# A graph and mixture-of-experts block on one core: places inside the inner products, both turns between the outer products, shared outer products evicted by ScalarE

## What is computed

```python
probs = jax.nn.softmax(flat @ Wr, axis=-1)            # flat: the normalized x, 625 by 768; 8 experts
topk_p, topk_i = jax.lax.top_k(probs, 2)
...
order = jnp.argsort(-score, axis=1)[:, :capacity]     # of each expert, its 196 best nodes
dispatch = flat[order]
gate = jax.nn.silu(jnp.einsum('ech,ehi->eci', dispatch, w1))     # 768 by 192 of each expert
up = jnp.einsum('ech,ehi->eci', dispatch, w3)
expert_out = jnp.einsum('eci,eih->ech', gate * up, w2)
...
shared = jax.nn.silu(flat @ s1) * (flat @ s3) @ s2
out = routed + shared
```

## Time and profile before

| | us |
|---|---|
| median of three runs | 1425.12 |
| the profiled execution's own time | 1431.91 |
| its span | 1430.3 |
| TensorE busy | 1311.4 |
| VectorE busy | 964.7 |
| ScalarE busy | 556.2 |
| GpSimd busy | 642.4 |
| mean granted TensorE clock, share of full | 0.946 |

### The profile page before, as it was taken

How to read it: one execution, slowest core, us unless ns; L and a number is a source line. 1 busy time by engine, 2 the same in 40 slices (tenths; PEclk the granted TensorE clock), 3 DMA queues, 4 the chain that set the end, 5 groups by cost and what they waited for, 6 DMA issues and landing times.

```text
span 1430.3 us, 22837 instructions
## 1 busy us (share of the span) xinstructions
PE 1311.4 (92%) x7548; PEld 1114.4 (78%) x7548; DVE 964.7 (67%) x2158; ACT 556.2 (39%) x652; POOL 642.4 (45%) x564
## 2 busy tenths in 40 slices
PE   7988678899999979999999999999999769988997
PEld 5765578556997769999999999999867559765665
DVE  8967998878689645565666656565168765477634
ACT  1010575231432044545454545454157551212221
POOL 7025777777666533344344434443368720001112
PEclk9999688999999889999999999999999889988988
DMA  7950000020740338787878787878588843416745
GB/s 174 87 46 6 2 2 2 1 67 3 215 96 2 101 135 293 259 279 272 279 279 288 264 291 263 300 252 280 132 282 279 281 152 96 133 32 167 178 118 173
DMA packets 116403, 234.59 MB, mean 164 GB/s; under 512 B 36931, under 2 KB 57087, under 8 KB 116301
## 3 DMA queue, kind: packets, MB, share of 16 engines
q1 hardware_dynamic: 80780, 126.83, 31.0%
q0 software_dynamic: 22352, 70.40, 17.4%
q10 hardware_dynamic: 13200, 36.46, 6.9%
HBM read 195.26 MB, written 39.70 MB: 164 GB/s over the span
## 4 chain that ended last, share of the span: by engine, by line
PE 63%; DVE 24%; issue 5%; DMA 4%; ACT 3%; POOL 1%; another core or an unknown queue 0%; DVEq 0%; ACTq 0%; SPq 0%; POOLq 0%
PE PS L2722 30%; PE PS L2387 4%; PE PS L2712 3%; PE PS L3007 3%; PE PS L2598 3%; PE PS L2996 3%; DVE e L1320 3%; DVE mlo L2162 3%; PE PS L2855 2%; PE PS L2897 2%; PE PS L2785 2%; DVE e L1562 2%; DVE e L1599 2%; PE PS L2817 1%; PE PS L2906 1%
## 5 line engine op out<-in xcount | busy, mean ns | idle before, releaser
L814 POOL DMA_INDIRECT xg<-xn_dram,xrow x70 | 116.1, 1658 | 277.6 <-DVEq L1529 245.4
L2722 PE MATMUL PS<-whi,xhi 128*128 128x384 f32 x840 | 220.7, 343 | 1.0 <-ACTq L1102 1.0
L2722 PE MATMUL PS<-whi,xlo 128*128 128x384 f32 x840 | 214.7, 336 | 0.0
L2722 PE MATMUL PS<-wlo,xhi 128*128 128x384 f32 x840 | 213.1, 335 | 0.0
L1320 DVE TENSOR_TENSOR wlo<-raw,whi 128x2304 fp32r<-128x2304 f32 x68 | 175.2, 2576 | 38.0 <-ACTq L1085 31.5
L1083 ACT ACTIVATE whi<-raw 128x2304 fp32r<-128x2304 f32 x68 | 145.1, 2133 | 22.8 <-PE PS L2694 7.8
L2722 PEld LDWEIGHTS PS<-wlo,xhi 128*128 128x128 f32 x840 | 151.8, 188 | 0.0
L2722 PEld LDWEIGHTS PS<-whi,xlo 128*128 128x128 f32 x840 | 151.7, 188 | 0.0
L1320 DVE TENSOR_TENSOR xlo<-PS,xhi 128x768 fp32r<-128x768 f32 x70 | 67.0, 958 | 124.1 <-ACTq L1094 117.2
L2722 PEld LDWEIGHTS PS<-whi,xhi 128*128 128x128 f32 x840 | 148.3, 189 | 1.3 <-issue 1.3
L782 POOL DMA_INDIRECT evwb<-inv_dram,idxb x80 | 108.2, 1352 | 30.5 <-issue 22.4
(11 more groups left out here) (463 smaller groups left out, 2671.2 us busy)
## 6 DMA issues: line engine op xcount, KB each, us to landing
raw<-in_L_gnn_W_rel SPq DMA_DIRECT2D x68, 1152.0 KB
z_dram<-xn ACTq DMA_DIRECT2D x70, 384.0 KB, 7.3
gw<-in_L_gnn_W SPq DMA_DIRECT2D x2, 2304.0 KB, 27.4
fw<-in_L_ffn_w SPq DMA_DIRECT2D x8, 576.0 KB
fw<-in_L_ffn_w ACTq DMA_DIRECT2D x1, 4608.0 KB
y_dram<-yb ACTq DMA_DIRECT2D x14, 294.0 KB
xn_dram<-xn SPq DMA_DIRECT2D x10, 384.0 KB
wroot<-in_L_ffn_w SPq DMA_DIRECT2D x5, 576.0 KB, 5.0
```

The costliest lines, as they stand in the source:

```text
L814: pool.indirect_dma_start(xg[b][j][:, :], None, xn_dram, bass.IndirectOffsetOnAxis(ap=xrow[:, b, j:j + 1], axis=0)).then_inc(x_gathered[b] ...
L2722: mm = pe.matmul(slot(q)[:, s * BANK:s * BANK + HALF], a[:, k, :], wt[:, k, s * HALF:(s + 1) * HALF], start=(k == 0 and part == 0), stop=( ...
```

## The change

- Before the experts, ScalarE loads Exp's table by an activation whose result nobody uses. The router's columns of the tiles 3 and 4 are made between the shared inner products.
- ScalarE evicts the shared outer products into `xn` (`shared_out`), and VectorE adds them to x from there, one in each of the experts 1 to 5.
- VectorE ranks expert n+2, not n+3, while expert n runs. Spreads run three experts ahead.
- In every expert the places of e+1 are made inside the inner product of e, ahead of its third part. The spread, and for the experts 5 and 6 `turn_hots`, stands between inner product and outer product 0. Both turns of e+1 stand between the two outer products, the first in slot 0, the second in slot 3.
- `row_tables` and `add_lower` are both done in expert 6. In the last stretch, `last_low(0)` comes before the first two `add_higher`.

```diff
--- before.py
+++ after.py
@@ -64,7 +64,9 @@
 SH = T
 HT = CAP // 2
 RING = 3
-SPREAD_AHEAD = 4
+SPREAD_AHEAD = 3
+X_SLOT = (0, 3)
+SHARED_SLOT = (0, 1, 2, 1, 2)
 LOGITS_WITH = 3
 PLACES = 768
 FINAL = NE - 1
...
@@ -1224,7 +1227,7 @@
 
             def take_x(n, j):
                 act.wait_ge(turned, n * RT + j + 1)
-                step.do(act.activation(fxT[n % 2][:, :, j * HT:(j + 1) * HT], columns2(0)[:, :, 0:HT], ACT.Copy))
+                step.do(act.activation(fxT[n % 2][:, :, j * HT:(j + 1) * HT], columns2(X_SLOT[j])[:, :, 0:HT], ACT.Copy))
                 act.sem_inc(x_taken, 1)
 
             def y_out(n, j):
@@ -1271,43 +1274,48 @@
                 step.do(act.activation(hhT[t % 2][:, :, 0:P], slot(3)[0:HC, BANK + 256:2 * BANK].rearrange("p (c n) -> p c n", c=2)[:, :, 0:P], ACT.Copy))
                 act.sem_inc(hT_ready, 1)
 
+            def shared_out(t):
+                act.wait_ge(outer_full, t + 1)
+                step.do(act.activation(xn[:, t, :].rearrange("p (b c) -> p b c", b=2),
+                                       slot(SHARED_SLOT[t]).rearrange("p (b c) -> p b c", c=BANK)[0:P, :, 0:HALF], ACT.Copy))
+                act.sem_inc(outer_taken, 1)
+
             for t in range(LOGITS_WITH):
                 shared_gate(t)
+            act.activation(table_of_exp[:, :], ones[0:P, 0:1], ACT.Exp)
             shared_turned(0)
             router(2)
             shared_gate(3)
             shared_turned(1)
+            score_row(0)
+            act.wait_ge(xn_stored, 32 * T)
+            shared_out(0)
             shared_gate(4)
-            score_row(0)
             shared_turned(2)
+            shared_out(1)
             shared_turned(3)
+            shared_out(2)
             score_row(1)
+            shared_out(3)
             shared_turned(4)
-            score_row(2)
             for j in range(RT):
                 take_x(0, j)
+            shared_out(4)
             for n in range(NE):
                 expert_gates(n)
-                if n < 2:
-                    if n == 1:
-                        score_row(4)
-                    for j in range(RT):
-                        y_out(n, j)
-                        take_x(n + 1, j)
-                    score_row(3 if n == 0 else n + SPREAD_AHEAD)
-                    continue
-                if n + 1 < NE:
-                    take_x(n + 1, 0)
+                if n == 0:
+                    score_row(2)
+                if n + SPREAD_AHEAD < NE:
+                    score_row(n + SPREAD_AHEAD)
+                elif FINAL - RT <= n < FINAL:
+                    hot_out(n - (FINAL - RT))
                 if n == FINAL:
                     for j in range(RT):
                         y_last(j)
                     continue
                 y_out(n, 0)
-                take_x(n + 1, 1)
-                if n + SPREAD_AHEAD < NE:
-                    score_row(n + SPREAD_AHEAD)
-                elif n >= FINAL - RT:
-                    hot_out(n - (FINAL - RT))
+                for j in range(RT):
+                    take_x(n + 1, j)
                 y_out(n, 1)
 
 
@@ -2206,13 +2214,9 @@
                 do(dve.tensor_copy(scol[e % 2][:, :], score[:, :, e]))
                 dve.sem_inc(scol_ready, 1)
 
-            SHARED_SLOT = (0, 1, 2, 1, 2)
-
             def add_shared(t):
-                dve.wait_ge(outer_full, t + 1)
-                xr = x_res[:, t, :].rearrange("p (b c) -> p b c", b=2)
-                do(tt(xr, slot(SHARED_SLOT[t]).rearrange("p (b c) -> p b c", c=BANK)[0:P, :, 0:HALF], xr, ALU.add))
-                dve.sem_inc(outer_taken, 1)
+                dve.wait_ge(outer_taken, t + 1)
+                do(tt(x_res[:, t, :], xn[:, t, :], x_res[:, t, :], ALU.add))
 
             def rank(e, first, end):
 
@@ -2291,51 +2295,28 @@
                 column2(e)
             do(dve.memset(level[:, 0, :], 0.0))
             shared_hidden(3)
-            shared_hidden(4)
             dve.wait_ge(earlier_ready, 1)
             rank(0, 0, 3)
-            add_shared(0)
-            add_shared(1)
+            shared_hidden(4)
             rank(0, 3, T)
             placed(0)
-            add_shared(2)
             rows2(0)
-            rank(1, 0, 2)
-            add_shared(3)
-            rank(1, 2, 4)
-            add_shared(4)
-            rank(1, 4, T)
+            rank(1, 0, T)
             placed(1)
-            hidden_rest(0)
-            hidden_first(0)
-            rows2(1)
-            rank(2, 0, T)
-            placed(2)
-            rank(3, 0, 3)
-            hidden_rest(1)
-            rows2(2)
-            hidden_first(1)
-            rank(3, 3, T)
-            placed(3)
-            rank(4, 0, 3)
-            rows2(3)
-            rank(4, 3, T)
-            placed(4)
             do(dve.tensor_copy(ident16[:, :], ident[0:P, 0:P]))
-            for n in range(2, NE):
-                if n == FINAL:
+            for n in range(NE):
+                hidden_rest(n)
+                if n + 1 < NE:
+                    rows2(n + 1)
+                hidden_first(n)
+                if n + 2 < NE:
+                    rank(n + 2, 0, T)
+                    placed(n + 2)
+                    if 0 < n:
+                        add_shared(n - 1)
+                elif n + 2 == NE:
+                    row_tables()
                     add_lower()
-                hidden_rest(n)
-                hidden_first(n)
-                if n + 3 < NE:
-                    rank(n + 3, 0, 3)
-                if n + 2 < NE:
-                    rows2(n + 2)
-                if n + 3 < NE:
-                    rank(n + 3, 3, T)
-                    placed(n + 3)
-                elif n + 3 == NE:
-                    row_tables()
 
             def add_higher(t):
                 dve.wait_ge(y_gathered[max(t - 1, 0)], 32 if t < 2 else 16)
@@ -2347,13 +2328,12 @@
                 lanes = lambda a: a[0:HT, :].rearrange("p (b c) -> p b c", b=2)
                 tt(lanes(y_split[1][j]), of, lanes(y_split[0][j]).bitcast(f32), ALU.subtract).then_inc(y_lo, 1)
 
+            last_low(0)
             add_higher(0)
             add_higher(1)
-            last_low(0)
-            add_higher(2)
             last_low(1)
-            add_higher(3)
-            add_higher(4)
+            for t in range(2, T):
+                add_higher(t)
             for t in range(T):
                 dve.wait_ge(joined, t + 1)
                 xr = x_res[:, t, :].rearrange("p (b c) -> p b c", b=2)
@@ -2907,15 +2887,15 @@
                                    start=(k == 0), stop=(k == K - 1))
                 mm.then_inc(inner_full, 1)
 
-            def last_logits():
+            def logits_alone(t):
                 pe.wait_ge(free[3], BEFORE["slot3"][3])
-                for t in range(LOGITS_WITH, T):
-                    pe.wait_ge(xT_ready, XT_TURNED[5] + t + 1)
-                    c = (t - LOGITS_WITH) * NE
-                    for k in range(K):
-                        mm = pe.matmul(slot(3)[0:P, c:c + NE], xT[:, k, t * P:(t + 1) * P], s13[:, k, 2 * F:2 * F + NE],
-                                       start=(k == 0), stop=(k == K - 1))
-                mm.then_inc(full[3], 1)
+                pe.wait_ge(xT_ready, XT_TURNED[5] + t + 1)
+                c = (t - LOGITS_WITH) * NE
+                for k in range(K):
+                    mm = pe.matmul(slot(3)[0:P, c:c + NE], xT[:, k, t * P:(t + 1) * P], s13[:, k, 2 * F:2 * F + NE],
+                                   start=(k == 0), stop=(k == K - 1))
+                if t == T - 1:
+                    mm.then_inc(full[3], 1)
 
             pe.wait_ge(split_lo, 2 * REL + SPLITS1 + K // 2)
             gcn_weight(0)
...
@@ -2976,10 +2956,12 @@
             def turn_x(e, j):
                 k = e * RT + j
                 pe.wait_ge(x_gathered[k % 4 // 2][k % 2], 16 * (REL // 2 + (k % 2 == 0) + k // 4 + 1))
-                if k:
-                    pe.wait_ge(x_taken, k)
+                if j == 1 and e > NE - SPREAD_AHEAD:
+                    pe.wait_ge(hots_ready, e - (NE - SPREAD_AHEAD))
+                elif j == 1:
+                    pe.wait_ge(srow_ready, e + SPREAD_AHEAD if e else 2)
                 for c in range(K):
-                    mm = pe.transpose(slot(0)[:, c * 128:c * 128 + HT], fx[k % 4][0:HT, c * 128:(c + 1) * 128], ident[0:HT, 0:HT])
+                    mm = pe.transpose(slot(X_SLOT[j])[:, c * 128:c * 128 + HT], fx[k % 4][0:HT, c * 128:(c + 1) * 128], ident[0:HT, 0:HT])
                 mm.then_inc(turned, 1)
 
             def inner_product(e, between=lambda: None):
@@ -3011,59 +2993,43 @@
             shared_turn(0)
             shared_inner(3)
             shared_turn(1)
-            shared_inner(4)
+            shared_outer(0, 0)
             pe.wait_ge(hT_ready, 2)
             pe.wait_ge(scol_ready, 1)
             spread(3, lambda t: scol[0][:, t:t + 1])
-            shared_outer(0, 0)
+            shared_inner(4)
             pe.wait_ge(srow_ready, 1)
             shared_turn(2)
```

(53 more changed lines are left out.)

## The result

The changed kernel takes **1449.05 us** (median of 4 runs, 1445.27 to 1451.54), the kernel before 1425.31 beside it (1415.44 to 1428.79). The ratio is 1.0172, 95% interval 1.0134 to 1.0211: slower by 1.7%. The time lies in the range (1417 to 1453), 11 us above the forecast of 1438. In the later comparisons the kernel before had medians of 1423.19 to 1426.82; a second one of the changed kernel gave 1450.82 and a ratio of 1.0203 (1.0178 to 1.0228).

What follows compares the result with a forecast made beforehand. After the change the second gather, behind weights in the DMA queues, and VectorE's late list and adds hold TensorE up. Terms -1.5 - 8.3 + 8.9 + 7.6 + 1.1 + 4.8 = +12.6 on 1425.12 give 1438 us, range 1417 to 1453.

Steps and rivals of the forecast that it cites:

- Where the waits come: TensorE idles 2 to 3.5 us before second turns of experts 2 to 5, 9 to 10 in expert 5, 5 before expert 7's outer products.
- One sign that I had named for being wrong: DMA queues: the prediction is wrong if the gathers' queue moves data while the weights do; no size given.
- The first rival: DMA queues, experts 1 to 4: second gather not held up, lands at 11.3; sum -5.4, 1420 us; chance 0.22.
- Unit of work: One expert after the change, from its inner product's start at full clock to outer product 1's end: 14.2 us.
- Expert 0: Second gather about level with the weights' request, taken as ahead of it: 15.5 us for 23.8, -8.3.
- the other end: Upper end for expert 0: 15.5 + 2.8 + 2.3 = 20.6 us.
- Experts 1 to 4: Second gather behind weights lands at 13.5, TensorE idles 2.8 us; 4 x (17.0 + 2.3) = 77.2 for 68.3, +8.9.
- Clock: TensorE's half clock after idle time: 2.3 us charged for each wait over 1.4, with ends of 0 and 4.9.
- Expert 5: `turn_hots` waits for VectorE's ranking of expert 7, ready at 16.8; with 2.3 of clock 26.6 us for 19.0, +7.6.
- The end: From inner product 7 on: tables and adds delay expert 7's products, outer products start after 11.9 us for 6.99; +4.8.
- First stage: Shared expert and router: three adds leave VectorE's way, table load moves off the router's path; between 0 and -3, taken -1.5.
- the third rival: Long half-clock stretches after each wait: 1448 us, or 1453 with expert 0 held up too; chance 0.15.

Runs made afterwards that it cites:

- The runs without the hold-up: Changed kernel with SyncE asking for expert e+3's weights only after both turns of expert e+1, 1420.82 us; the same after the first turn, 1422.10 us.
- The run with 29 and 19 filling products: Changed kernel with 29 and 19 TensorE products nobody reads, made while it would wait for expert 7's list and before expert 7's outer products: 1439.76 us, ratio 1.0103.

## Why the prediction was right, and where its sizes were not

- **Where the waits come: right.** The second gather in experts 1 to 4, the list in expert 5, the adds before expert 7, all ended by what was named. One sign that I had named for being wrong did appear: the gathers' queue moved data while the weights did. The waits came all the same, so the sign was badly chosen; sharing holds a gather up too. The first rival (the gather not held up, 1420) did not come. The runs without the hold-up lie 2.4 and 3.1 us below the kernel before beside them, where that rival had 5.4, so its sum was about right and its condition was not. In part that is luck: its experts 0 to 4 came out 2.4 us shorter (72.3 for 74.7), and it had the clock behind the two long waits too small, as the forecast had. The Trainium skill, "DMA: Bandwidth & Descriptors", section "Queues, rings and completion order", says that a DMA engine takes turns between its queues packet by packet. The slices above agree in part, since both queues do move together there, and not for the slice with 381 packets of weights against 4 of gathers; what it was taken to mean, that the gather hardly suffers, is refuted by 6.5 to 6.9 us against 4.2.
- **Unit of work: right.** 14.2 worked out, 14.3 to 14.8 measured where nothing waits.
- **Expert 0: the step that failed.** "I take it as ahead." The gather was ahead of the weights by 0.57 us, and that was not enough: 20.20 us, where the other end said 20.6. That costs 4.7 us of the sum. The error was to ask for the order of the requests, where what counts is how far apart they are.
- **Experts 1 to 4: two sizes off, in one direction.** Waits of 9.6 us in all for 11.2. The gather was not the reason: it took 6.5 to 6.9 us, and 6.6 had been put in (13.5 - 6.87). In experts 2 and 3 the first turn ended 11.0 us after the inner product's start for 10.7, and the gather landed at 13.3 for 13.5. Clock: charged four times, 9.2 us in all, it came once in this execution and cost 4.4 there, since it reached into the next inner product, and 1.5 more came over from expert 0. Over the 40 waits of eight profiles it cost 2.3 us a wait, so as a mean the charge was sound.
- **Expert 5: the wait right, the clock too small.** The list was ready 1379.73 + 0.99 - 1363.80 = 16.9 us after inner product 5 began, for 16.8. But what follows took 5.5 us more than at full clock, not 2.3. The 2.3 came from an idle time of 4.46 us; behind 10.28 us TensorE stayed at half clock through two outer products and two turns.
- **The end: the same.** The outer products began 13.1 us after inner product 7 for 11.9, and took 10.31 us for 5.91. I had put 1.2 us for the clock between ends of 0 and 2.3; it was 4.4. The run with 29 and 19 filling products shows these two clock terms, 10 us together, by the experiment.
- **First stage**: -2.5, inside 0 to -3. The early table load, put at nothing, brings the first places 0.87 us earlier, and no gain of the whole that the run could show.

With expert 0 held up (+4.7) and the clock behind the two long waits (+3.2 and +3.2) the sum is 12.6 + 11.1 = 23.7 us, and the medians lie 23.7 apart. That the two agree to the digit is luck: in the single profile, experts 1 to 4 are 4.1 below their term and the earlier part 3.2 shorter. The time is also that of the third rival, 1448 to 1453, but long low stretches did not come behind each wait, as it says, but behind some of them and both long ones.

## What to carry to other kernels

When a move brings a small gather and a large load within a microsecond of each other, compare not their order but their distance, and put the load where the gather has landed: one added wait was worth 2% of the changed kernel. In the kernel before, the same wait brought nothing; its profile shows the load next to other gathers. Charge an idle TensorE twice, for the wait and for the clock behind it, and let the second grow with the first; 17 us of waiting cost some 10 us more here. And when a rotation shortens the main loop, look at each one-time piece of work that was placed by the old one (a list, a table, a round of adds): two such pieces cost 17 and 7 us of a change whose loop itself had 20 us to give.

## What the runs showed of the hardware that was not expected

- A semaphore whose increment stands behind two indirect DMAs in GpSimd's order was raised 1.50 us before the second one's instruction began in the trace (1.04 for the first expert, 1.50 for the seven others). It does not mark that a request has been written, or even begun.
- The second of two gathers of 98 rows took 4.0 to 4.8 us to land alone and 6.2 to 7.6 beside 1.15 MB of weights, also where it was asked for 0.57 us ahead of them. The first, 1.3 us ahead of them, took 3.7 to 4.5.
- Idle times of 1.6 to 3.4 us were followed by half clock in 30 of 40 cases, with no length that divides them. Idle times of 6.8 to 8.0 us before the last outer products were followed by it each time and cost 1.5 to 4.4 us more, those of 10.3 us in expert 5 cost 4 to 6 us more, and 9 in the second profile of the changed kernel, where half clock lasted into the next inner product.
